# A twelve-stage decoder kernel: the context's rotation moved into a later stage, the first attention's decays as a square, a reordered cross attention of layer 0, and a query rotation packed to 128 partitions

## Chip, cores and metric

The program runs on one core of one Trainium2 chip. The metric is the device time of one execution in microseconds (us). Engines are called PE (TensorE), DVE (VectorE), ACT (ScalarE), POOL (GpSimd) and SP (SyncE, which issues most transfers). All large arithmetic is fp32.

## The reference, cut to what matters

A decoder of four layers with three sublayers each, every one of the form `x = x + f(layernorm(x))`, for x of (4, 256, 256) and a context of (4, 512, 64). The change touches five of them.

```python
# L0_attn: 16 heads of 16, chunks of 128, decay per head
D = exp(ld[:, None, None] * where(mask, diff, 0)) * mask
q_decay = exp(ld[None, :] * (idx + 1)[:, None])
k_decay = exp(ld[None, :] * (chunk - 1 - idx)[:, None])
scores = einsum('bchd,bshd->bhcs', qb, kb) * D[None]
# L0_xattn: 16 heads of 16, causal, on the context's first 256 rows
scores = where(causal, einsum('bhqd,bhkd->bhqk', qh, kh) / sqrt(16), finfo.min)
out = einsum('bhqk,bhkd->bhqd', softmax(scores), vh) @ Wout.T
# L1_xattn: 16 heads; both the query (192 wide) and the context (64 wide) are rotated
q_big = einsum('bshk,hkq->bshq', (hidden_q @ Wq.T).reshape(..., H, K), w_kc_q)
q_big = q_big * cos_q + rotate_half(q_big) * sin_q
kv_r = kv_c * cos_k + rotate_half(kv_c) * sin_k
scores = einsum('bhsr,bhlr->bhsl', einsum('bshq,hqr->bhsr', q_big, W_qr),
                einsum('bld,hdr->bhlr', kv_r, W_kr))
ctx_c = einsum('bhsl,bld->bhsd', softmax(scores), kv_r)
```

L1_attn (a selective scan over 96 channels with a second layernorm and a convolution ahead) is not changed in what it computes. L2_xattn and L3_xattn use the rotated context too.

## The kernel before

The stages run one after another, from `STAGES` in `program` (L3369 on). A stage is a row of blocks (`k.block()`); a block holds one list of instructions for each engine, ordered by semaphores, and ends when all its lists have ended. Ahead of each stage stands `layernorm` (L220 to L251), whose block also issues the stage's first transfers on SP (`fetch`, through `load`, L318). Inside a list an engine works strictly in the order written; nothing is reordered by a planner.

**The context.** `rotate_context` is a block of its own ahead of all stages: three transfers (L1510 to L1512), 13 DVE operations (L1519 to L1523) that rotate the context into `keys`, 16 transposes on PE (L1533), and two DVE copies (L1526) into `keysT`. Its results are first read in L1_xattn.

**L0_attn.** DVE builds the exponents `arg` (L592 to L596, 2320 columns). ACT takes `powers = exp(arg/8)` (L523) and its logarithm (L524), then Tanh of the query projections (L530), then Silu of the rest (L532, L537, L541). DVE corrects `powers` by one Newton step (L599, L601) and squares it three times (L603, L604, L605), scales the key's part (L607, `decay_done` 2) and builds the table (L608); only then it makes the queries, four times L613, L616, L617. PE's projections (L405, L413) go through 6 PSUM banks: the seventh waits until the first query has been taken (`took_q`). Behind them stand the low-rank gate projection (L418), which waits for no bank, its second half (L424), which waits for DVE's copy L619, and the state products (L430), which wait for POOL's L567 and L571; POOL waits for `decay_done`. The loop over 16 half units is L451 to L500.

**L0_xattn.** After 20 projections a loop over 16 steps s (4 batches x 4 groups of 4 heads), software pipelined by two. For each half step, 2 heads: `scores` writes two causal masks by bf16 matmuls (L742) and the scores by fp32 matmuls of 32 partitions (L756); DVE takes row maxima (L840); PE transposes them (`turn_tops`, L766); DVE adds them to the queries (`lower`, L849); `scores_again` computes the transposed scores with the maximum taken off (L742 again, L784); ACT takes exponentials (L892, 768 columns); `values` multiplies them with the values (L795, four column groups of 32) ; ACT keeps the sums (L898); `turn_sums` transposes them (L807) and DVE normalises (L856, L857), all inside the loop. `project_out` follows.

**L1_attn, first block.** DVE: second layernorm (L1335 to L1347), scaling out of PSUM (L1354), convolution (L1361 to L1364), the gate's product (L1369, L1371), a copy (L1374). PE: transposes (L1410), input projection (L1416), two small projections (L1421, L1425). ACT: Tanh (L1397), later Abs, Exp, Ln. POOL has nothing there. In the loop behind it POOL adds (L1477) while DVE works (L198 and on).

**L1_xattn (`latent_attention` with `rope`).** A block folds weights: `Cm` from W_qr and W_kr (L1604, 32 matmuls), `Bm` (L1612), and `Em` (L1625) in four groups, taken out of PSUM by ACT (L1655, L1658) and DVE (L1668, L1671). Weights "first" and "second" are fetched in the layernorm's block, "third" to "fifth" in this one. The next block rotates: 32 items m (8 head pairs x 2 column halves x 2 heads). `widen(m)` makes two halves of 96 rows of a head's query (L1696, 4 matmuls), DVE multiplies them with cosines and sines (L1730, L1732, 4 operations of 96x512), `narrow(m)` contracts the four products to 64 rows (L1707, 4 matmuls); the two heads of a pair follow one another. The loop is `widen(m)`, then `narrow(m-1)`:

```python
for m in range(len(items) + 1):
    if m < len(items):
        widen(m)
    if m >= 1:
        narrow(m - 1)
```

ACT copies the result to `qT` (L1741). The attention over the context follows (L1796 to L1915) and is the same code in L2_xattn and L3_xattn.

## Time and profile before

| what | us |
|---|---|
| median of 3 runs | 3408.3 |
| the runs | 3388.36, 3408.3, 3412.52 |
| the profiled execution, its own time | 3433.46 |
| its span, first to last instruction | 3431.6 |
| mean granted TensorE clock over the span | 0.819 |
| PE, DVE, ACT, POOL busy | 2704.5, 1804.5, 981.2, 799.5 |

The profile is of one execution. "Busy" is the time in which an engine executes; matmuls are pipelined and their ends are modelled, so that starts are the safer reading. PEclk is the granted clock as a share of 2.4 GHz; its two levels are 1.00 and 0.50. L12 is line 12 of the kernel before. An fp32 matmul appears as two MATMUL rows. In brackets stands how long the engine sat idle before the instruction and what ended that.

### The profile page before, as it was taken

The page shows a single profiled execution, that of the slowest core. Times are in us where ns is not written, and L with a number is a line of the kernel's source. Part 1 is how long each engine was busy: PE and PEld are TensorE (multiplying, and loading weights), DVE is VectorE, ACT ScalarE, POOL GpSimd, SP SyncE. Part 2 cuts the span into 40 slices and gives each one's busy share as a digit, 9 for nine tenths or more (in the row PEclk, how much of TensorE's full clock was granted, in tenths as well). Part 3 has the DMA queues.
Part 4 walks back from the last instruction along what each step waited for, and adds up shares of the span by engine and source line. Part 5 has one row for each costly group of instructions (what it writes and reads, how often), then busy time and mean ns, then how long its engine had stood idle before and what let it go on. Part 6 is the DMA issues. An engine that isn't in the chain of part 4 may idle for free. (4 is left out here: it accounts for less than half of the span.)

```text
span 3431.6 us, 37431 instructions
## 1 busy us (share of the span) xinstructions
PE 2704.5 (79%) x14214; PEld 1753.0 (51%) x14214; DVE 1804.5 (53%) x3596; ACT 981.2 (29%) x2209; POOL 799.5 (23%) x565
## 2 busy tenths in 40 slices
PE   4799634265999998967787869688998765899899
PEld 2555332122433555545676757475555744555555
DVE  5422568698333655348475665742554755255511
ACT  2121101153000554113423333331554111255410
POOL 1130000022000886220000000000885000188422
PEclk9765556566999999978787878877999975799899
DMA  1000000001100001021000000102001001100211
GB/s 39 16 18 1 19 0 1 3 0 48 43 0 0 1 1 51 1 100 23 3 13 13 13 13 1 25 21 66 1 1 38 0 18 44 42 1 1 77 50 40
DMA packets 96634, 72.72 MB, mean 21 GB/s; under 512 B 51248, under 2 KB 89952, under 8 KB 95881
## 3 DMA queue, kind: packets, MB, share of 16 engines
q1 hardware_dynamic: 95433, 68.88, 7.2%
q8 instruction: 114, 1.87, 0.2%
q0 software_dynamic: 1024, 1.45, 0.2%
q14 instruction: 63, 0.52, 0.0%
HBM read 65.04 MB, written 5.28 MB: 20 GB/s over the span
## 5 line engine op out<-in xcount | busy, mean ns | idle before, releaser
L1915 POOL TENSOR_SCALAR work<-work,small 128x512 f32<-128x512 f32 x384 | 593.1, 1562 | 912.3 <-DVE small L1851 912.1
L1893 ACT ACTIVATE work<-psum,small 128x512 f32<-128x512 f32 x384 | 260.2, 683 | 251.7 <-DVE small L1846 251.7
L1846 DVE TENSOR_REDUCE small<-psum 128x2 f32<-128x1024 f32 x192 | 234.8, 1224 | 178.3 <-PE psum L1796 178.2
L1796 PE MATMUL psum<-keysT,arena_a 64*128 64x512 f32 x768 | 217.1, 644 | 9.1 <-ACT work L1893 6.2
L1806 PEld LDWEIGHTS psum<-consts,work 128*128 128x128 f32 x1536 | 164.5, 141 | 114.8 <-issue 99.9
L1806 PE MATMUL psum<-consts,work 128*128 128x128 f32 x1536 | 210.9, 280 | 5.4 <-DVE work L1857 2.6
L1818 PE MATMUL psum<-work,keys 128*64 128x256 f32 x1536 | 186.9, 384 | 35.3 <-issue 34.0
L1818 PEld LDWEIGHTS psum<-work,keys 128*64 128x64 f32 x1536 | 120.0, 136 | 135.1 <-issue 109.1
L2704 PE MATMUL psum<-xnT,arena_a 128*128 128x256 f32 x512 | 154.4, 463 | 29.1 <-DVE arena_b L3084 29.1
L1477 POOL TENSOR_TENSOR arena_b<-arena_b 96x1024 f32<-96x1024 f32 x16 | 37.6, 2348 | 591.3 <-DVE arena_b L1470 591.3
L1441 PE MATMUL psum<-arena_b,arena_a 96*96 96x512 f32 x128 | 92.8, 895 | 72.5 <-DVE arena_b L1470 38.1
L2704 PEld LDWEIGHTS psum<-xnT,arena_a 128*128 128x128 f32 x512 | 117.1, 237 | 55.7 <-DVE arena_b L3084 31.2
L1857 DVE COPY work<-psum 128x512 f32<-128x512 f32 x192 | 130.7, 681 | 19.8 <-PE psum L1806 19.8
L1730 DVE TENSOR_TENSOR arena_a<-psum,work 96x512 f32<-96x512 f32 x96 | 62.8, 681 | 146.0 <-PE psum L1696 146.0
L2677 POOL TENSOR_TENSOR work<-arena_b 128x512 f32<-128x512 f32 x32 | 33.3, 1039 | 439.6 <-ACT arena_b L2965 408.5
L1900 ACT ACTIVATE work<-psum 128x512 f32<-128x512 f32 x192 | 114.3, 595 | 73.1 <-PE psum L1806 73.1
L2281 PE MATMUL psum<-xnT,arena_b 128*128 128x512 f32 (+1 forms) x272 | 121.7, 601 | 0.0
L1696 PE MATMUL psum<-xnT,arena_b 128*96 128x512 f32 x256 | 117.3, 601 | 1.6 <-PEq L72 1.6
L1707 PE MATMUL psum<-arena_a,arena_b 96*64 96x512 f32 x256 | 115.7, 598 | 0.0
L251 PE MATMUL psum<-consts,xn 128*128 128x128 f32 x192 | 43.7, 420 | 86.7 <-DVE xn L232 86.7
L840 DVE TENSOR_REDUCE work<-psum 128x2 f32<-128x256 f32 x64 | 32.7, 554 | 134.2 <-PE psum L756 134.2
L3084 DVE SCALAR_TENSOR_TENSOR work<-psum,conv_w,work 128x255 f32<-128x255 f32 (+2 forms) x192 | 83.1, 476 | 36.7 <-ACT work L2959 34.1
(576 smaller groups left out, 5222.5 us busy)
## 6 DMA issues: line engine op xcount, KB each, us to landing
arena_a<-in_L_xattn_Wo SPq DMA_DIRECT2D x3, 2048.0 KB, 12.5
arena_a<-in_L_xattn_Wq SPq DMA_DIRECT2D x3, 2048.0 KB, 17.5
arena_a<-in_L_xattn_w_kc_q SPq DMA_DIRECT2D x3, 1536.0 KB, 11.7
arena_a<-in_L_attn_w_qkv SPq DMA_DIRECT2D x1, 4096.0 KB
arena_a<-in_L_xattn_W_qr SPq DMA_DIRECT2D x3, 768.0 KB
arena_b<-in_L_ffn_w_fc SPq DMA_DIRECT2D x1, 2048.0 KB
arena_b<-in_L_ffn_w_proj SPq DMA_DIRECT2D x1, 2048.0 KB
arena_a<-in_L_attn_w_gate SPq DMA_DIRECT2D x1, 2048.0 KB
```

The source lines that it names most:

```text
L1696: mm = nc.tensor.matmul(ps[0:QH, m % 2 * 2 + q, :], Em[:, c, 2 * i + j, q * QH:(q + 1) * QH], xnT[:, c, n * 512:(n + 1) * 512], start=c == ...
L1707: mm = nc.tensor.matmul(ps[j * DC:(j + 1) * DC, 4 + g % 4, :], Cm[:, c_at(2 * i + j), z // 2, :], prods[m % 2][:, z, :], start=z == 0, sto ...
L1796: mm = nc.tensor.matmul(ps[:, u % 2 * 2 + j, :], qT[r:r + DC, p, t * P:(t + 1) * P], k.keysT[r:r + DC, b * SK:(b + 1) * SK], start=True, s ...
L1806: mm = nc.tensor.transpose(ps[:, 4 + j, c * P:(c + 1) * P], probs[u % NPB][:, j, c * P:(c + 1) * P], k.c["ident"])
L1818: mm = nc.tensor.matmul(ps[j * DC:(j + 1) * DC, 6, 0:S], k.keys[:, 4 * b + c, :], PT[q % 2][:, j, c], start=c == 0, stop=c == 3)
L1846: nc.vector.tensor_reduce(top[:, 2 * u:2 * u + 2], ps[:, u % 2 * 2:u % 2 * 2 + 2, :], AX.X, ALU.max, negate=True).then_inc(*maxed.up())
L1857: nc.vector.tensor_copy(PT[u // 2 % 2][:, 0, :, u % 2, :], ps[:, 4, :].rearrange("p (c n) -> p c n", c=4)).then_inc(*kept_d.up())
L1893: nc.scalar.activation(probs[u % NPB][:, j, :], ps[:, u % 2 * 2 + j, :], ACT.Exp, bias=top[:, i:i + 1], accum_out=total[:, i:i + 1]).then_ ...
L1900: nc.scalar.activation(PT[u // 2 % 2][:, 1, :, u % 2, :], ps[:, 5, :].rearrange("p (c n) -> p c n", c=4), ACT.Copy).then_inc(*kept_a.up())
L1915: nc.gpsimd.tensor_scalar(probs[u % NPB][:, j, :], probs[u % NPB][:, j, :], total[:, i:i + 1], None, ALU.mult).then_inc(*scaled.up())
L2281: mm = nc.tensor.matmul(ps[0:n_f, 4 + g % 2 * 2 + z, :], gu[:, c, z, i * P:i * P + n_f], xnT[:, c, n * 512:(n + 1) * 512], start=c == 0, s ...
L2704: mm = nc.tensor.matmul(ps[:, n % 3, j * S:(j + 1) * S], w_qkv[:, c, f:f + P], xnT[:, c, b * S:(b + 1) * S], start=c == 0, stop=c == 1)
```

## The change

Five edits in one.

- The context is no longer rotated in a block of its own. Its three transfers are issued in the layernorm of L1_attn behind that stage's own; POOL does the 13 operations in L1_attn's first block (`context_rotate`), PE the 16 transposes behind the input projection (`context_turn`), ACT two copies of 64x2048 behind Tanh (`context_keep`); the third small projection waits for them.
- L0_attn: `powers = exp(arg/2)`, squared once. ACT's four Tanh stand ahead of Exp and Ln, DVE's query operations ahead of the decays, and the square, `k_decay` and the table behind the copy of the gate.
- L0_xattn: scores of step s and scores again of step s-2 are issued together, alternately, on four different row groups; masks of both ahead. PSUM banks have fixed roles; `values` writes 128 columns a matmul (three a head instead of two). The sums are kept for all steps and transposed and normalised in a block behind the loop.
- L1_xattn, fold: `Cm` becomes `CmA` (128 rows) and `CmB` (64 rows), from a rearranged copy `w_cut` of W_qr that POOL makes; `Bm` is computed first; `Em` is written in two parts.
- L1_xattn, rotation: 16 units (head pair, column half) with three banks: 128 of the 192 rows of each head, and the remaining 64 rows of both heads together. 6 matmuls, 6 DVE operations of 128x512 with a table that has the sign in it, 8 narrow matmuls that alternate between the two heads' column halves.

```diff
@@ L0_attn, ACT
-            act.wait_ge(*decays.at(1))
-            k.link(act, nc.scalar.activation(powers, arg, ACT.Exp, scale=0.125), "act")
+            for i in range(4):
+                act.wait_ge(*proj.at(i + 1))
+                nc.scalar.activation(q[...], ps[:, i % 6, :], ACT.Tanh, scale=0.5).then_inc(*tanhed.up())
+            act.wait_ge(*decays.at(1))
+            k.link(act, nc.scalar.activation(powers, arg, ACT.Exp, scale=0.5), "act")
...
@@ L0_attn, DVE, behind the four query groups
+            dve.wait_ge(*k.sig("logs").at(1))
+            (arg = 0.5 * arg - logs; powers = (arg + 1) * powers)
             dve.wait_ge(*low.at(1))
             nc.vector.tensor_copy(t1..., ps[0:HD, 6:8, :]).then_inc(*put.up())
+            nc.vector.tensor_tensor(powers, powers, powers, ALU.mult).then_inc(*k.sig("decay_done").up())
+            (k_decay, decay_done; table)
@@ L0_xattn, PE
+            def both(s, half):
+                ask, again = s < Q, 0 <= s - 2 < Q
+                q, other = s - 2, 1 - half
+                first, second = FIRST[half], SECOND[other]
+                if ask:
+                    b, g = divmod(s, G)
+                    if s >= 1:
+                        pe.wait_ge(*maxed.at(2 * (s - 1) + half + 1))
+                    if half == 1 and s >= 1:
+                        pe.wait_ge(*lowered.at(s))
+                    for j in range(2):
+                        hide_later(first + j, 0)
+                if again:
+                    if q >= 1:
+                        pe.wait_ge(*expd.at(2 * (q - 1) + half + 1))
+                    if other == 0 and s >= 3:
+                        pe.wait_ge(*kept.at(s - 2))
+                    pe.wait_ge(*lowered.at(q + 1))
+                    for j in range(2):
+                        hide_later(second + j, 1)
+                for i in range(2):
+                    for j in range(2):
+                        if ask:
+                            r, (a, e), t0 = 64 * half + 32 * j, ((0, 1), (1, 3))[i], b * S
+                            mm = nc.tensor.matmul(ps[:, first + j, a * P:e * P], qT[r:r + 32, ...], kT[r:r + 32, ...], ...)
+                        if again:
+                            r, (a, e), t0 = 64 * other + 32 * j, ((0, 2), (2, 3))[i], q // G * S
+                            mm = nc.tensor.matmul(ps[:, second + j, a * P:e * P], kT[r:r + 32, ...], low_q[q % 3][r:r + 32, ...], ...)
+            for s in range(Q + 3):
+                both(s, 0)
+                if s >= 3:
+                    values(s - 3)
                 if 1 <= s <= Q:
                     turn_tops(s - 1)
+                both(s, 1)
...
@@ L1_attn, first block
             act: nc.scalar.activation(u, conv, ACT.Tanh, scale=0.5)
+            context_keep(k, act)
             pe: (input projection)
+            context_turn(k, pe)
             pe.wait_ge(*lowed.at(1))
+            pe.wait_ge(*k.sig("keys_kept").at(1))
+        @block.gpsimd
+        def _(pool):
+            context_rotate(k, pool)
@@ L1_xattn, rotation, PE
+                def widen(u):
+                    for bank, col in ((0, 0), (2, 2 * P), (1, P)):
+                        for c in range(2):
+                            mm = nc.tensor.matmul(ps[:, u % 2 * 3 + bank, :], Em[:, c, i, col:col + P],
+                                                  xnT[:, c, n * 512:(n + 1) * 512], start=c == 0, stop=c == 1)
+                def narrow(u):
+                    for v in range(2):
+                        for j in range(2):
+                            nc.tensor.matmul(ps[j * DC:(j + 1) * DC, 6 + u % 2, :], CmA[:, c_at(2 * i + j), v, :],
+                                             prods[u % 2][:, j, v, :], start=v == 0, stop=False)
+                    for v in range(2):
+                        for j in range(2):
+                            r = slice(j * DC, (j + 1) * DC)
+                            mm = nc.tensor.matmul(ps[r, 6 + u % 2, :], CmB[r, i, v, :], prods[u % 2][r, 2, v, :],
+                                                  start=False, stop=v == 1)
```

## Rows read from the trace of the kernel before

**Rows 1.** The page, section 1: busy time, share of the span and instructions of each engine.
```profile
PE 2704.5 (79%) x14214; PEld 1753.0 (51%) x14214; DVE 1804.5 (53%) x3596; ACT 981.2 (29%) x2209; POOL 799.5 (23%) x565
```
**Rows 2.** Busy time by stretches: length, PE, PEld, DVE, ACT, POOL, PEclk, DMA share, GB/s.
```profile
128.00:136.00 8.00, 7.45 (x74) 5.15 (x72) 5.44 (x6) 0.63 (x1) 0.00 (x0) 1.00 0.01 2
187.30:197.90 10.60, 10.59 (x33) 5.90 (x32) 0.69 (x1) 7.29 (x11) 8.16 (x9) 1.00 0.23 62
198.60:378.60 180.00, 176.78 (x960) 96.78 (x960) 44.75 (x112) 33.31 (x49) 6.88 (x7) 0.50 0.02 5
...
884.40:1113.90 229.50, 228.75 (x512) 71.49 (x512) 79.38 (x128) 9.55 (x16) 0.00 (x0) 1.00 0.00 0
1113.90:1356.00 242.10, 223.95 (x1408) 135.01 (x1408) 140.88 (x230) 129.02 (x322) 197.69 (x128) 1.00 0.00 1
```
**Rows 3.** Timeline of the rotation, one item: start, duration, engine, line, shapes, count.
```profile
1002.75 3.67 PE L1696 MATMUL psum<-xnT,arena_b 128*96 128x512 f32 x8
...
1006.36 3.65 PE L1707 MATMUL psum<-arena_a,arena_b 96*64 96x512 f32 x8
```
**Rows 4.** Timeline, the context's block: its first transfer, and the first of the next stage.
```profile
6.99 0.37 SPq L1510 DMA_DIRECT2D work<-in_ctx  x1
...
25.25 0.34 SPq L318 DMA_DIRECT2D arena_a<-in_L_attn_log_decay  x1
```
**Rows 5.** Timeline of L1_attn: its first block, and L198 alone and beside POOL.
```profile
644.99 1.06 ACT L1397 ACTIVATE arena_b<-arena_a 96x1024 f32<-96x1024 f32 x1 [19.84 <-DVE arena_a L1364]
...
653.11 3.72 PE L1425 MATMUL psum<-arena_a 6*96 6x512 f32 x4 [1.37 <-DVE arena_a L1374]
...
699.31 1.28 DVE L198 SCALAR_TENSOR_TENSOR work<-arena_b,arena_a,work 96x1024 f32<-96x1024 f32 x1
...
825.34 2.34 POOL L1477 TENSOR_TENSOR arena_b<-arena_b 96x1024 f32<-96x1024 f32 x1 [6.20 <-DVE arena_b L1470]
826.36 2.40 DVE L198 SCALAR_TENSOR_TENSOR work<-arena_b,arena_a,work 96x1024 f32<-96x1024 f32 x1
```
**Rows 6.** Timeline of L0_attn around the projections.
```profile
35.92 10.54 PE L405 MATMUL psum<-xnT,arena_a 128*128 128x512 f32 x24 [1.05 <-PEq L72]
...
44.40 2.23 ACT L524 ACTIVATE arena_a<-arena_a,consts 128x2320 f32<-128x2320 f32 x1
...
51.87 2.58 DVE L603 TENSOR_TENSOR arena_a<-arena_a 128x2320 f32<-128x2320 f32 x1
...
62.85 5.30 PE L405 MATMUL psum<-xnT,arena_a 128*128 128x512 f32 x8 [16.39 <-DVE arena_b L613]
...
82.08 1.21 DVE L619 COPY arena_b<-psum 16x1024 f32<-16x1024 f32 x1 [11.74 <-PE psum L418]
...
87.31 3.78 PE L430 MATMUL psum<-work 128*128 128x128 f32 x16
```
**Rows 7.** Timeline of L0_xattn's loop, parts of a step.
```profile
300.87 0.61 PE L742 MATMUL psum<-arena_b 128*128 128x256 bf16 x2
...
301.40 1.65 PE L756 MATMUL psum<-arena_a 32*128 32x128 f32 x8
...
303.60 1.51 PE L795 MATMUL psum<-work,arena_a 128*32 128x256 f32 x16
...
304.04 0.41 DVE L849 TENSOR_TENSOR work<-psum,arena_a 128x256 f32<-128x256 f32 x1
```
**Rows 8.** Timeline of L0_attn's loop: the same kind of pair in the stretch from 128 us.
```profile
131.07 1.13 PE L451 MATMUL psum<-arena_a,work 32*128 32x256 f32 x8
```
**Rows 9.** Timeline of L1_xattn's attention, PE alone.
```profile
1200.27 1.95 PE L1818 MATMUL psum<-work,keys 128*64 128x256 f32 x16 [0.39 <-issue]
...
1203.17 1.13 PE L1796 MATMUL psum<-keysT,arena_a 64*128 64x512 f32 x4
```
**Rows 10.** Timeline of L1_xattn's fold, two PE groups.
```profile
854.13 5.41 PE L1604 MATMUL psum<-arena_a 64*96 64x64 f32 x64 [1.05 <-PEq L72]
...
869.37 13.44 PE L1625 MATMUL psum<-arena_a 128*128 128x192 f32 x64 [5.29 <-issue]
```

More of the change, by code:

```diff
@@ L1607, in _, with outputs @@
-            mm.then_inc(*fold.up())
-            k.wait_weights(pe, "second")
-            for h in range(H):
-                r, i = h % 2 * DC, h // 2
-                mm = nc.tensor.matmul(ps[r:r + DC, 4 + i // 2, i % 2 * D:(i % 2 + 1) * D], w_v[:, h, :], wo[:, h, :],
-                                      start=True, stop=True)
-            mm.then_inc(*fold.up())
+            def outputs():
+                k.wait_weights(pe, "second")
+                for h in range(H):
+                    r, i = h % 2 * DC, h // 2
+                    mm = nc.tensor.matmul(ps[r:r + DC, 4 + i // 2, i % 2 * D:(i % 2 + 1) * D], w_v[:, h, :], wo[:, h, :],
+                                          start=True, stop=True)
+                mm.then_inc(*fold.up())
@@ new lines, in _ @@
+            k.wait_weights(pe, "first")
+            if rope:
+                outputs()
+                pe.wait_ge(*k.sig("ready").at(1))
+                for h in range(H):
+                    r, a = h % 2 * R, c_at(h)
+                    for v in range(2):
+                        mm = nc.tensor.matmul(ps[:, a // 4, (a % 4 * 2 + v) * DC:(a % 4 * 2 + v + 1) * DC],
+                                              w_cut[r:r + R, h // 2, v, 0:P], w_kr[r:r + R, h // 2, :], start=True, stop=True)
+                mm.then_inc(*fold.up())
+                pe.wait_ge(*taken.at(1))
+                for h in range(H):
+                    r, a = h % 2 * R, h // 2
+                    for v in range(2):
+                        mm = nc.tensor.matmul(ps[r:r + R, 4 + a // 4, (a % 4 * 2 + v) * DC:(a % 4 * 2 + v + 1) * DC],
+                                              w_cut[r:r + R, h // 2, v, P:Q], w_kr[r:r + R, h // 2, :], start=True, stop=True)
+                mm.then_inc(*fold.up())
+            else:
+                for h in range(H):
+                    r = h % 2 * R
+                    for c in range(2):
+                        a = c_at(h)
+                        mm = nc.tensor.matmul(ps[0:QH, a // 4, (a % 4 * 2 + c) * DC:(a % 4 * 2 + c + 1) * DC],
+                                              w_qr[r:r + R, h // 2, c * QH:(c + 1) * QH], w_kr[r:r + R, h // 2, :],
+                                              start=True, stop=True)
+                mm.then_inc(*fold.up())
+                outputs()
@@ L1645, in _ @@
                 mm.then_inc(*fold.up())
+        if rope:
+            @block.gpsimd
+            def _(pool):
+                k.wait_weights(pool, "first")
+                halves = w_qr.rearrange("p h (z d) -> p h z d", z=2)
+                for v in range(2):
+                    for z in range(2):
+                        nc.gpsimd.tensor_copy(w_cut[:, :, v, 64 * z:64 * z + 64], halves[:, :, (z + v) % 2, 0:64])
+                        last = nc.gpsimd.tensor_copy(w_cut[:, :, v, P + 32 * z:P + 32 * z + 32], halves[:, :, (z + v) % 2, 64:QH])
+                last.then_inc(*k.sig("ready").up())
         @block.scalar
@@ L1680, in latent_attention @@
     if rope:
-        prods = [A.take(QH, 4, 512) for _ in range(2)]
+        prods = [A.take(P, 3, 2, 512) for _ in range(2)]
         rotated = k.sig("rotated")
+        units = [divmod(u, 2) for u in range(2 * HP)]
         with k.block() as block:
@@ L1686, in _ @@
             def _(pe):
-                items = [(i, n, j) for i in range(HP) for n in range(2) for j in range(2)]
-                def widen(m):
-                    i, n, j = items[m]
-                    if m >= 2:
-                        pe.wait_ge(*rotated.at(m - 1))
-                    for q in range(2):
+                def widen(u):
+                    i, n = units[u]
+                    if u >= 2:
+                        pe.wait_ge(*rotated.at(u - 1))
+                    for bank, col in ((0, 0), (2, 2 * P), (1, P)):
@@ L1717, in _ @@
+                for u in range(2 * HP + 1):
+                    if u < 2 * HP:
+                        widen(u)
+                    if u >= 1:
+                        narrow(u - 1)
             @block.vector
@@ L1737, in _ @@
             def _(act):
[L1738 to L1742 removed]
+                for u in range(2 * HP):
+                    i, n = units[u]
+                    act.wait_ge(*k.sig("mm_out").at(u + 1))
+                    nc.scalar.activation(qT[:, i, n * 512:(n + 1) * 512], ps[:, 6 + u % 2, :], ACT.Copy).then_inc(*taken.up())
     else:
```

377 lines of the change are left out of this document (159 added, 218 removed).

## Prediction

> **What bounds the kernel now.** I read the page first, then the busy time by stretches, then the order of instructions in the five places that the diff touches. The page shows no engine that is the limit everywhere: PE is busy 79% of the span, DVE 53% [rows 1]. The program is twelve stages, each with blocks that end in a barrier, so the average says little; each edit has to be priced in its own stage, between the barriers that close it. Two of the five places are waits: from 6.99 to 25.25 us the context's rotation, a block of its own behind which all stages stand [rows 4], and 16.4 us in L0_attn in which PE is idle and DVE's L613 ends it [rows 6]. The other two show in the stretches [rows 2]: from 198.6 to 378.6 us (cross attention of layer 0) PE is busy 176.8 of 180.0 us, at a granted clock of 0.50 throughout, the lower level, 1.2 GHz. In 884.4 to 1113.9 us (rotation of the queries of layer 1) PE is busy 228.75 of 229.5 us at 1.00, 2.4 GHz, and DVE only 79.4. So there PE's own instructions are the bound, and only fewer, or more of them side by side, or a higher clock can shorten them.
>
> A measure used below: an fp32 matmul is two MATMUL rows. Eight rows of 512 columns, one after the other, take 3.61 us to the start of the next group [rows 3]; I put 0.43 each, 3.44, down to streaming (0.84 ns a column at 2.4 GHz, so 1.67 ns at 1.2 GHz) and the other 0.17 us to the change of shape.
>
> **Part 1, the context.** Its block ran from 6.99 to 25.25 us [rows 4], with nothing else in it; the next stage starts 18.3 us earlier. What it did goes into the first block of L1_attn and its layernorm. Three transfers are added behind eleven others on SP's queue; that queue has nothing else to do in the layernorm. POOL gets 13 instructions. 96x1024 takes it 2.34 us [rows 5], so I estimate 0.6 us for each of 4 of 256 elements, 0.3 for each of 8 of 128, 2.3 for the last: 7.1 us, from the block's start at about 620 to 628. PE's 16 transposes (3.8 us like the 16 of L430, [rows 6]) stand behind the input projection, while DVE does its convolution, which ends at 645.0. ACT's two copies of 64x2048 (I estimate 1.9 us each, from 1.06 for 1024 columns) stand behind Tanh, 646.05 to 649.9; the matmul that waits for them would start at 653.11 [rows 5]. All hidden, with some 3 us to spare. What is not hidden is POOL beside DVE: the same DVE instruction takes 1.28 us alone and 2.40 us while POOL works [rows 5]. DVE's chain of small operations in the second layernorm lies just there. I take 1.5 us; the ends are 0 and POOL's whole 7.1. A gain is possible too: 16 more transposes may let PE's two 3.6 us groups run at 2.4 GHz, up to 3.6 us. Term: -16.8 (from -22 to -11).
> The Trainium skill, SBUF — State Buffer, "Who interferes with whom", speaks against this placement: a DVE instruction with two SBUF inputs and a GpSimd instruction that reads SBUF exclude each other for a whole instruction. By that rule the loss is at most POOL's own time, so a term between -18.3 and -11.2; the 1.28 against 2.40 us agree with it.
>
> **Part 2, the decays.** Now ACT's Tanh for the queries stands behind Exp and Ln (2.2 us each), and DVE's product behind five operations of 2320 columns (2.58 us each) and the table; PE waits 16.39 us for DVE's L613 [rows 6]. After: the sixth projection ends at 46.4 (six in 10.54 us, 1.72 each), and by then DVE, free since 39.6 when the exponents are made, has taken the first query and freed the seventh's bank. The next wait could be for the key's Silu: Tanh until 43.5, then Exp, Ln and three table loads (I estimate 1.3 each from the gaps between them), Silu at 52.3; PE needs that bank at 53.1. So PE runs through 14 projections and the low-rank one (3.6) to 63.7, where it now ends at 82.05 [rows 6]. What is late next is POOL's key decay: PE needs the two squares' result through decay_done. DVE: copy 63.7 to 65.0, one square to 67.6, then POOL's two products of 1024 columns, 2.34 each by the row of L1477 [rows 5], to about 72.3. PE's L430, which started at 87.31, starts at about 72.3: 15.0 us. POOL's first product and DVE's table (2.3) now overlap and may cost each other a microsecond or two; if ACT's path slips it costs as much. Term: -15 (from -17 to -11). Of the two dropped multiplications (5.2 us) only one would have lain on this path.
>
> **Part 3, cross attention of layer 0.** Its 16 steps with their ends take 180.0 us, 11.25 each [rows 2]. L756 (32 partitions, two row groups) is 4x128+4x256 columns, 2.57 us if serial; it took 1.65 [rows 7], so its two row groups run side by side (1.28). L795 is (8x256+8x128) columns, 5.1 us serial, and took 1.51: four column groups side by side. The change issues four row groups together, two of `ask`, two of `again`, 384 columns each. A half then costs four masks (0.21 each at 1.2 GHz by their 256 bf16 columns, 0.85) + 1.28 + about 0.4 for changes of shape = 2.5 us, in place of two halves of 2.1 (L742 to L756 0.53, L756 1.6, [rows 7]). A step at 1.2 GHz: 2x2.5, values 1.5, tops 0.6, and a wait that is new: the second half's masks wait for lower(), which waits for the tops just issued, 0.1+0.41+0.1 = 0.6 us. Together 7.8 us. At 2.4 GHz by the shapes that ran there (8 rows of L451 in 1.13 us where two side by side stream 0.86, [rows 8]): half 0.43+0.64+0.3 = 1.37, values 0.85 (half of 1.5 and 0.1), tops 0.45, wait 0.6: 4.7 us. DVE (44.75/16 = 2.8 us a step now) and ACT (33.31/16 = 2.1) stay below either [rows 2].
> Which clock? PE was busy all along at 1.2 GHz with two row groups; with one group of 64 rows (187.3 to 197.9) and with pairs that fill the array (1113.9 to 1356) it was at 2.4 [rows 2]. The new step does the same work in 70% of the time even at 1.2 GHz, so I take 2.4 after the first steps. Loop: 17 steps' worth x 4.7 = 80, first steps at the lower clock 11, and the new block behind it (32 transposes, four pairs of DVE operations, a barrier) an estimated 7, from 3.8 us for 16 such [rows 6]: 98 against 180. Term: -82 (from -97, all at 2.4, to +5, below).
> The Trainium skill, TensorE: Matmul & The Clock Gate, Part 3, "Measured speedup vs the span model", gives 3.07, not 4, for four row groups. By that 0.64 becomes 0.83 and the term -75 (an estimate of mine from that page). No run here shows four row groups together.
>
> **Part 4, rotation of layer 1.** Before: 229.5 us for 32 items, 7.17 each, of which widen 3.61 and narrow 3.56 [rows 3]. After: 16 units; widen 12 rows at 0.43 = 5.16; narrow 8 rows with 128 partitions by 64 columns and 8 of 64 by 64, each in pairs on different halves. L1818 has the first shape: 16 rows of 256 columns, 3.45 us serial, 1.95 measured; L1796 has row pairs: 1.13 us where serial is 1.72 [rows 9]. So 1.72+1.72, and three changes of shape 0.45: 9.05 us, x16 = 145. DVE has 79.38/128 = 0.62 us an operation, 6 a unit, 3.7 us, and is hidden [rows 2]. Term: -84 (serial pairs: 12.5 us, 200, -29; at best -87).
> In front of it the fold grows. CmA's weights have 128 columns where L1604's have 96, at 5.41/64 = 0.085 us each [rows 10]; 64 x 0.11 = 7.2 us, CmB 64 x 0.058 = 3.7, together 10.9 in place of 5.4. Now PE waits 5.29 us for weights, until 869.37; after, outputs() can start when Wo has landed (by 859.5, when L1604 ends and its matmuls run now; I take 858), takes 4.6, then 10.9: 873.5. POOL's w_cut (8 copies, about 4 us) is hidden behind outputs(). With split evacuations +4 (from +1 to +6).
>
> **Sum.** -16.8 -15 -82 -84 +4 = -194 us. The profiled execution took 3433.5 us (span 3431.6), so 3239.5 for it; it was 25 us above the median of the three runs, 3408.3, for which the same sum gives **3214 us**.
>
> **Rivals.**
> (A) The loop of layer 0 stays at 1.2 GHz. For: it never left 0.50 in 180 us. Against: the work is now denser. 17x7.8+9 = 142, term -38: 3258 us. 20%.
> (B) The 64-column pairs of the rotation run one after another, since the 512-column form and the mix of three shapes in a unit are not in the trace. Term -29: 3269 us. 7%.
> (C) The change doesn't do what it says: four row groups in the order j, j' don't overlap, only two do. Half 3.8 us at 1.2 GHz, step 10.3, 175+10 = 185, +5: 3301 us. 7%.
> (D) Slower: the narrow shapes in the rotation let the clock fall, and it stays down through the attention behind it. At 1.2 GHz a unit takes 17.6 us, 282 (+52), and the 242.1 us of attention, with PE busy 224, lose up to 200: 3214+84+52+200 = 3550 us. With the other terms it turns slower once the attention loses over some 58 us, a quarter of its stretch at 1.2 GHz. Against: the same shapes held 1.00 [rows 2]. 2%.
> My forecast 64%. The range 3175 to 3285 holds it, A and B and the bounds of parts 1 and 2; C, D and a still better loop are left out. A measurement of this kernel tells about 1%, 34 us, from no change; all but D and an odd remainder are faster by more: 0.96, 0.02, 0.02.
>
> **What would show it.** Right: first stage's DMA issue at 7 us; no PE idle of 16 us near 30 to 45; a step of about 4.7 us in the layer 0 loop with PEclk 1.00; rotation of about 145 us with L1818-like pairs; w_dt's matmul in L1_attn not waiting for ACT. Wrong: a loop step of 8 us or more, a narrow part over 4 us, or a rotation below clock 1.00.

## The result, and the profile after it

| | before | after |
|---|---|---|
| median of the runs, us | 3410.41 (4 runs, 3388.36 to 3430.91) | 3240.18 (4 runs, 3237.0 to 3245.44) |
| ratio, 95% interval | | 0.9503 (0.9442 to 0.9565) |
| the profiled execution, us | 3433.46 (span 3431.6) | 3245.44 (span 3243.6) |
| mean granted clock of it | 0.819 | 0.829 |

170 us less by the medians, 188 by the profiled executions (after's profiled execution is one of its four runs, before's is a fifth). Every stage begins with its first transfer on SP, so the starts of those rows split both spans (in us; the last column is what the prediction gave):

| stage | before | after | difference | predicted |
|---|---|---|---|---|
| ahead of L0_attn | 25.25 | 7.25 | -18.0 | -18.3 |
| L0_attn | 134.25 | 121.78 | -12.5 | -15 |
| L0_xattn | 231.50 | 144.80 | -86.7 | -82 |
| L1_attn | 234.01 | 237.72 | +3.7 | +1.5 |
| L1_xattn | 511.92 | 427.55 | -84.4 | -84 +4 |
| the eight others | 2294.67 | 2304.50 | +9.8 | 0 |
| span | 3431.60 | 3243.60 | -188.0 | -194 |

The stages that the diff doesn't touch are 9.8 us longer in this one execution (L2_attn 3.9, L2_xattn 2.9, L3_ffn 2.0 of it). In the fourteen profiles of this study, those of the experiments below included, the same code in L2_attn took 816.05 to 823.33 us. That is the size of what one profile can't tell.

The page of after, section 1, and the busy time of the loop of layer 0 (its first steps, the rest, the new block behind it), of the rotation and of the attention (columns as in [rows 2]):

```profile
PE 2533.6 (78%) x14342; PEld 1696.4 (52%) x14342; DVE 1770.8 (55%) x3533; ACT 985.2 (30%) x2219; POOL 814.6 (25%) x586
...
168.44:188.22 19.78, 17.96 (x130) 10.38 (x131) 7.37 (x16) 3.95 (x5) 6.90 (x7) 0.57 0.14 37
188.22:254.90 66.68, 57.78 (x926) 41.08 (x926) 30.86 (x65) 28.34 (x43) 0.00 (x0) 1.00 0.01 2
255.66:263.62 7.96, 6.54 (x32) 6.33 (x33) 4.20 (x8) 0.00 (x0) 0.00 (x0) 0.63 0.00 0
769.98:916.10 146.12, 145.18 (x448) 50.55 (x448) 58.90 (x96) 9.58 (x16) 0.00 (x0) 1.00 0.00 1
916.10:1158.20 242.10, 225.16 (x1408) 135.42 (x1408) 140.37 (x228) 128.69 (x321) 198.03 (x128) 0.99 0.00 1
```

Against [rows 2]: the loop, 180.0 us at 0.50, is now 95.2 us with its block, at 1.00 after the first 20 us up to the block behind it; the rotation, 229.5, is 146.1. The attention behind the rotation took 242.1 us in both, at 1.00 before and 0.99 after.

The timeline of a step of that loop, which answers to [rows 7] (behind each L741 row sixteen rows of 32 partitions are left out, two for each of the eight matmuls of a half step):

```profile
225.49 0.60 PE L741 MATMUL psum<-arena_b 128*128 128x256 bf16 x4 [0.61 <-DVE work L835]
...
226.89 0.61 PE L741 MATMUL psum<-arena_b 128*128 128x256 bf16 x4
...
228.29 0.66 PE L789 MATMUL psum<-work,arena_a 128*32 128x128 f32 x16
228.75 0.42 PE L793 MATMUL psum<-work,arena_a 128*32 128x128 f32 x8
229.11 0.44 PE L801 MATMUL psum<-consts,work 128*128 128x128 f32 x2
229.58 0.42 DVE L835 TENSOR_TENSOR work<-psum,arena_a 128x256 f32<-128x256 f32 x1 [1.55 <-PE psum L801]
...
230.15 0.60 PE L741 MATMUL psum<-arena_b 128*128 128x256 bf16 x4 [0.61 <-DVE work L835]
```

From L741 to L741 the step is 4.66 us: halves of 1.40, values 0.82, tops 0.44, and 0.61 in which PE waits for `lower` (L835).

L0_attn, the timeline that answers to [rows 6]:

```profile
17.91 16.30 PE L407 MATMUL psum<-xnT,arena_a 128*128 128x512 f32 x32 [1.05 <-PEq L72]
...
44.50 3.61 PE L420 MATMUL psum<-xnT,arena_a 128*16 128x512 f32 x8
...
48.22 1.21 DVE L613 COPY arena_b<-psum 16x1024 f32<-16x1024 f32 x1 [9.46 <-PE psum L420]
...
52.03 2.28 DVE L617 SCALAR_TENSOR_TENSOR arena_a<-arena_a 128x2048 f32<-128x2048 f32 x1
52.21 4.31 POOL L568 TENSOR_TENSOR work<-arena_b,arena_a 128x1024 f32<-128x1024 f32 x1 [29.82 <-DVE arena_a L616]
...
56.48 1.93 POOL L572 TENSOR_TENSOR work<-work,arena_a 128x1024 f32<-128x1024 f32 x1
58.46 3.78 PE L432 MATMUL psum<-work 128*128 128x128 f32 x16 [5.27 <-POOL work L572]
```

The wait of 16.39 us is gone. What is late now is POOL: PE's state products (L432, before L430) wait for L572, and L568, one operation of 128x1024, took 4.31 us beside DVE's table. DVE itself had idled 9.46 us in front of its copy L613.

L1_attn, first block: DVE's last small operations of the second layernorm, beside POOL's last of the context:

```profile
509.29 0.37 DVE L192 TENSOR_TENSOR ln_rs<-ln_rs 128x8 f32<-128x8 f32 x1
509.70 0.17 DVE L193 TENSOR_TENSOR ln_rs<-ln_rs 128x8 f32<-128x8 f32 x1
509.72 2.35 POOL L1318 TENSOR_TENSOR keys<-keys,work 128x1024 f32<-128x1024 f32 x1
509.90 2.19 DVE L1385 SCALAR_TENSOR_TENSOR ln_rs<-ln_mv,ln_rs 128x8 f32<-128x8 f32 x1
```

An operation of 8 elements a partition took 2.19 us, and it ended with POOL's.

The fold, which answers to [rows 10], and one unit of the rotation, which answers to [rows 3]:

```profile
746.66 5.12 PE L1620 MATMUL psum<-arena_a 128*64 128x256 f32 x32 [6.76 <-DMA arena_a<-in_L_xattn_Wo]
751.72 3.84 PE L1631 MATMUL psum<-arena_a,work 64*128 64x64 f32 x64
...
755.48 2.13 PE L1638 MATMUL psum<-arena_a,work 64*64 64x64 f32 x64
757.54 10.67 PE L1662 MATMUL psum<-arena_a 128*128 128x192 f32 x64
...
784.18 5.42 PE L1744 MATMUL psum<-xnT,arena_b 128*128 128x512 f32 x12
...
789.52 1.94 PE L1755 MATMUL psum<-arena_a,arena_b 128*64 128x512 f32 x8
...
791.39 1.93 PE L1760 MATMUL psum<-arena_a,arena_b 64*64 64x512 f32 x8
793.25 5.42 PE L1744 MATMUL psum<-xnT,arena_b 128*128 128x512 f32 x12
```

A unit is 9.07 us. CmA (L1631) took 3.84 us and CmB (L1638) 2.13.

### The profile page after: what moved, and what is told of

It reads as the page before. It is cut to its first block and busy times, and to the rows that moved or that the text cites. A ratio compares the mean times of both kernels' runs of the same rounds, so it can differ in the third digit from the quotient of the medians.

```text
span 3243.6 us, 37597 instructions
## 1 busy us (share of the span) xinstructions
PE 2533.6 (78%) x14342; PEld 1696.4 (52%) x14342; DVE 1770.8 (55%) x3533; ACT 985.2 (30%) x2219; POOL 814.6 (25%) x586
## 5 line engine op out<-in xcount | busy, mean ns | idle before, releaser
L1779 DVE TENSOR_TENSOR arena_a<-psum,work 128x512 f32<-128x512 f32 x96 | 58.9, 683 | 82.8 <-PE psum L1744 82.8
L2384 DVE TENSOR_TENSOR arena_a<-arena_a,psum 128x512 f32<-128x512 f32 (+1 forms) x34 | 23.4, 687 | 144.0 <-ACT arena_a L2406 144.0
L1489 PEld LDWEIGHTS psum<-arena_b,arena_a 96*96 96x96 f32 x128 | 29.9, 245 | 135.9 <-issue 84.8
L1877 PE MATMUL psum<-arena_b,work 128*128 128x256 f32 x384 | 99.1, 381 | 1.6 <-DVE work L1913 1.6
L1913 DVE COPY work<-psum 128x256 f32<-128x256 f32 x96 | 40.8, 425 | 108.8 <-PE psum L1867 108.8
```

What stands on the lines that cost most here:

```text
L1489: mm = nc.tensor.matmul(ps[0:C, s % 2 * 4 + 2 * g + n, :], w, u[:, n * 512:(n + 1) * 512], start=True, stop=True)
L1877: mm = nc.tensor.matmul(ps[:, 7, t * D:(t + 1) * D], ctx[q % 2][:, t * P:(t + 1) * P], Bm[:, p, :], start=p == 0 and t == 0, stop=p == HP ...
```

## Experiments

Every run is compared with runs of the kernel before on the same chip. The kernels stand in three groups that shared those runs, with medians of before of 3388.0, 3404.4 and 3395.7 us; after itself (3240.18) is from a fourth. The ratios below compare with before. After ran beside none of these kernels, so a total that lies within 5 us of 3240.18 is not taken as a difference from it; what an edit of after did is read from its own stage, against the same stage in the profiles in which that code is as in after.

### The kernel before once more

No edit.

> The kernel before, not changed, for a second profile. The profiled execution of before took 3433 us, 23 above the median of its four runs, and the stages that the diff doesn't touch took 9.7 us less in it than in the profile of after. Theory 1: the spread is the granted clock's, spread over the stages: the five stages of the diff repeat within 3 us each (context 18, L0_attn 134.3, L0_xattn 231.5, L1_attn 234.0, L1_xattn 511.9), and what the total differs by is in others. Theory 2: the loop of L0_xattn, at 1.2 GHz throughout in the first profile, gets the higher clock for a part in the shorter executions: then its 180 us come out 15 to 25 shorter and the median's gain of 170 us, against 188 in the profiles, is explained by it.

Measured: one execution, 3434.93 us, its stages within 0.9 us of the first profile's, L0_xattn 231.60 again. The profiled executions are alike, so this run tells neither theory from the other. But the seven other executions on that chip took 3372.74 to 3434.54 us: there is something in before that goes two ways, and both profiles show the longer one.

### Part 3 undone, and part 3 alone

The function `l0_xattn` of before put into after (first), and that of after put into before (second).

> After, with the cross attention of layer 0 as before (part 3 undone, all else as in after). Both profiles of before took 3433 to 3435 us, with the loop at a granted clock of 0.50 throughout, while other executions of before took 3373 to 3412; after's lie within 3237 to 3245. Theory 1: the loop of before is what can go either way: this kernel's executions spread over 40 us or more, up to 3245+87 = 3332 (loop 180 us at 1.2 GHz) and down to about 3270 to 3290; if the profiled one is a short one, its loop shows a clock above 0.50. Theory 2: the loop is always at 1.2 GHz and the spread of before is elsewhere: all executions within 10 us of 3327. Part 3 is then worth 87 us in every execution, by theory 1 only 30 to 60 in the shorter ones.

> Before, with the cross attention of layer 0 of after and nothing else (part 3 alone). By the stages of the two profiles 3433-87 = 3346 us. Theory 1 (the loop was what spread): executions within 10 us of 3346. Theory 2 (the spread is elsewhere): they spread over 40 us or more, 3285 to 3346, as those of before do.

Measured, part 3 undone: median 3301.88 us, 3277.61 to 3322.96 in six runs, ratio to before 0.9665 (0.9594 to 0.9736). The mean clock of those executions was 0.815 to 0.817 in the three long ones and 0.823 to 0.827 in the three short ones. The profiled one (3314.95) shows the loop, and for the first time a rise in it:

```profile
168.00:320.00 152.00, 151.16 (x818) 82.89 (x818) 38.59 (x95) 26.92 (x40) 5.18 (x6) 0.50 0.02 5
320.00:340.00 20.00, 17.19 (x135) 9.93 (x134) 5.63 (x16) 5.21 (x8) 0.00 (x0) 0.76 0.00 1
```

L0_xattn took 225.17 us in it, 6 less than in before. Part 3 alone: median 3354.58, all four within 3352.03 to 3358.93, ratio 0.9832 (0.9757 to 0.9907).

So the spread goes with the old loop: the kernels that have it spread over 42 to 72 us, those with the new one over 5 to 11. The old loop was at 0.50 throughout in two profiles and rose late in a third; the new one came to 1.00 within 25 us of its start in all ten profiles that have its masks ahead, and stayed there up to its last steps. Part 3 is worth 87 us against an execution whose loop stays at 1.2 GHz. By the medians it is worth less: 62 us with part 3 undone (3301.9 to 3240.2, two groups), 60 against the next kernel below, which has the new loop and shared the runs of before, and 50 with part 3 alone (3404.4 to 3354.6, the same chip). No profile of a short execution of before was had; that its gain lies in this loop rests on the two spreads and on this one rise.

### Two row groups at a time

```diff
                 for i in range(2):
                     for j in range(2):
                         if ask:
...
+                for i in range(2):
+                    for j in range(2):
                         if again:
                             (scores again)
```

> After, with the four matmuls of the scores issued ahead of the four of the scores again in each half step, so that neighbours lie on two row groups, no longer four. Same work, same number of instructions. Theory 1 (overlap reaches only over what is issued next to one another, and the denser step is what held the clock up): two groups at a time, the loop falls to 1.2 GHz, half 3.8 us, step about 10.3, L0_xattn 144.8+90 = 235, total 3330. Theory 2 (overlap as in theory 1, but the clock stays up): half 0.7 us longer at 2.4 GHz, step 6.1, L0_xattn 168, total 3263. Theory 3 (the second pair starts beside the first all the same, because their row groups differ): step under 5 us, no change.

Measured: 3242.11 us, ratio 0.9496 (0.9423 to 0.9569), L0_xattn 145.17. Theory 3. The timeline of a half step (L768 scores, L777 scores again; in the program all eight rows of L768 stand first):

```profile
222.23 0.38 PE L768 MATMUL psum<-arena_a 32*128 32x128 f32 x2
222.25 0.48 PE L777 MATMUL psum<-work,arena_a 32*128 32x256 f32 x2
222.44 0.49 PE L768 MATMUL psum<-arena_a 32*128 32x128 f32 x4
222.57 0.38 PE L777 MATMUL psum<-work,arena_a 32*128 32x256 f32 x2
```

The fifth instruction (the first L777) started 0.02 us behind the first and 0.2 ahead of the L768 rows that follow the first two. By these starts PE took matmuls of other row groups out of their order, so the alternation that the change writes out isn't what makes four run together. The section on the kernel before says that inside a list an engine works strictly in the order written; for PE's matmuls that doesn't hold.

### Masks between, as before

```diff
-                if again:
...
-                    for j in range(2):
-                        hide_later(second + j, 1)
                 for i in range(2):
                     for j in range(2):
                         if ask:
...
+                if again:
...
+                    for j in range(2):
+                        hide_later(second + j, 1)
+                for i in range(2):
+                    for j in range(2):
                         if again:
```

The three waits of scores again went with its masks to behind the first four matmuls.

> After, with the order of before inside a half step: masks and scores of the one step, then masks and scores again of the other. The run with two groups in turn showed that order among the eight 32-row matmuls doesn't matter (the fifth instruction started 20 ns behind the first); what is left that could keep four groups apart is a matmul of 128 rows between them. Theory 1 (masks of both ahead are what lets four groups overlap, and the denser step is what lifts the clock): half 0.7 us longer at 2.4 GHz and the clock falls, step 10 to 11, L0_xattn about 230, total 3325 with executions spread over 30 us or more, as with the old loop. Theory 2 (overlap lost, clock stays): step 6.1, L0_xattn 168, total 3263. Theory 3 (PE starts the second pair past the masks): no change, 3240.

Measured: 3343.29 us (3338.16 to 3345.92), ratio 0.9856 (0.9791 to 0.9921), L0_xattn 244.19. The half step in the timeline, and the loop's stretch:

```profile
200.68 0.59 PE L741 MATMUL psum<-arena_b 128*128 128x256 bf16 x2 [0.61 <-DVE work L837]
201.19 1.65 PE L760 MATMUL psum<-arena_a 32*128 32x128 f32 x8
202.78 0.61 PE L741 MATMUL psum<-arena_b 128*128 128x256 bf16 x2
203.31 1.65 PE L777 MATMUL psum<-work,arena_a 32*128 32x256 f32 x8
204.90 0.61 PE L741 MATMUL psum<-arena_b 128*128 128x256 bf16 x2
...
168.00:346.00 178.00, 162.62 (x990) 93.31 (x990) 38.21 (x80) 30.95 (x46) 6.93 (x8) 0.50 0.02 5
```

Theory 1 for the time: the pairs run one after the other, as in [rows 7], the step is 11.2 us and the clock stays at its lower level. Its spread of 30 us did not come (8 us), so a loop at 0.50 doesn't by itself bring the spread. With the run above this names the edit inside part 3 that pays: the masks, matmuls of 128 rows, no longer stand between those that are to overlap. The waits moved with the masks. The rows show no idle time at them, but a kernel with only the masks moved wasn't run, so that the masks alone end the overlap is not shown. The clock went with the overlap: the same matmuls ran at 0.50 pair after pair and at 1.00 four together.

### The rotation's pairs in turn

```diff
-                    for v in range(2):
-                        for j in range(2):
+                    for j in range(2):
+                        for v in range(2):
```

(in both groups of `narrow`)

> After, with the rotation's narrow matmuls ordered by head first: each head's two halves of a product one after the other on the same 64 columns, in place of alternating between the heads' column halves. Theory 1 (the gain of part 4 in narrow comes from neighbours on different column halves): each of the two groups of 8 rows goes from 1.94 to 3.45 us, the unit from 9.07 to 12.1, L1_xattn 427.5+49 = 476, total 3290. Theory 2: half of the neighbours still differ (j changes once in each group), so a part overlaps all the same: unit 11 to 11.5. Theory 3: order doesn't matter: 9.07.

Measured: 3239.43 us in one execution, and in the timeline

```profile
852.43 1.95 PE L1755 MATMUL psum<-arena_a,arena_b 128*64 128x512 f32 x8
...
854.31 1.94 PE L1760 MATMUL psum<-arena_a,arena_b 64*64 64x512 f32 x8
856.18 5.42 PE L1744 MATMUL psum<-xnT,arena_b 128*128 128x512 f32 x12
```

Theory 3. Had only neighbours on different column halves overlapped, a group would have taken longer than the 1.94 us of after; so column halves, too, are taken out of order, inferred from the time alone.

### Transposes of the maxima ahead of the values

```diff
+                if 1 <= s <= Q:
+                    turn_tops(s - 1)
                 if s >= 3:
                     values(s - 3)
-                if 1 <= s <= Q:
-                    turn_tops(s - 1)
```

> After, with the transposes of the maxima issued ahead of the values in each step of the layer 0 loop, so that the 0.8 us of values cover DVE's lower. PE idled 0.61 us a step for lower, 15 times. Theory 1: the step falls from 4.66 to 4.05 us, L0_xattn 144.8 to about 135, total 3230. Theory 2 (maxed isn't ready that early and PE waits there instead): under 3 us. Theory 3: with the step shorter ACT's exponentials (2x0.8 + 0.4 us and their latencies) become the bound: 3 to 7 us.

Measured: 3237.65 us (3234.54 to 3241.34), ratio 0.9577 (0.9546 to 0.9608), L0_xattn 141.14, 3.7 less than in after and below the 144.6 to 151.2 of all profiles with after's loop. The step is 4.36 us (L801 at 222.01 and 226.37). The wait for `lower` is gone, but 0.2 to 0.3 us of another took its place: half of the masks wait until ACT has copied the sums of `values` out of PSUM (L870, 0.38 us), and `values` now stands right ahead of them. No theory had it; the size is that of theory 2.

### Squares early, and the eighth power kept

The first moves DVE's square, key decay and table ahead of the wait for the low-rank projection. The second keeps after's order and takes back the power:

```diff
-            k.link(act, nc.scalar.activation(powers, arg, ACT.Exp, scale=0.5), "act")
+            k.link(act, nc.scalar.activation(powers, arg, ACT.Exp, scale=0.125), "act")
...
+            k.link(dve, nc.vector.tensor_tensor(powers, powers, powers, ALU.mult), "dve")
+            k.link(dve, nc.vector.tensor_tensor(powers, powers, powers, ALU.mult), "dve")
             dve.wait_ge(*low.at(1))
```

(and 0.125 for 0.5 in the Newton step).

> After, with DVE's square, key decay and table moved from behind the copy of the gate to ahead of its wait. DVE idled 9.46 us in front of that copy. Theory 1 (the decays were late only by their place in DVE's order): decay_done comes at about 41.5 instead of 52.1, POOL's two products are done by about 48, and the state products start straight behind the gate's second half, 53.2 instead of 58.46: 5.3 us less in L0_attn, total 3235. Theory 2 (the end of the stage is set by the loop behind it, where the clock is low and PE waits for others): L0_attn shorter by under 2 us. Theory 3: POOL beside DVE slows DVE's copy, so that the low-rank part is late: no gain.

> After, with the decays as an eighth power again (scale 0.125, two more squarings of 2320 columns on DVE, 2.57 us each) but in after's order, the two ahead of the wait for the low-rank projection, where DVE idled 9.46 us. Theory 1 (the gain of part 2 was all from the order): the state products start as in after, 51.2 us into the stage (48.6 where the clock is up from the first projection), total 3240 within 3. Theory 2 (as the prediction had it: one of the two dropped squarings lay on the path): 2.6 us later. Theory 3: both, 5.2 us later, 3245.

Measured, squares early: 3236.53 us (3233.21 to 3238.68), ratio 0.9577 (0.9549 to 0.9606).

```profile
41.47 4.32 POOL L568 TENSOR_TENSOR work<-arena_b,arena_a 128x1024 f32<-128x1024 f32 x1 [19.34 <-DVE arena_a L614]
45.75 1.93 POOL L572 TENSOR_TENSOR work<-work,arena_a 128x1024 f32<-128x1024 f32 x1
...
52.92 3.57 PE L432 MATMUL psum<-work 128*128 128x128 f32 x16
```

The stage began at 7.01, so L432 came 45.9 us into it in place of 51.2: the 5.3 us of theory 1. The stage got 3.0 shorter (118.75), and that isn't separated from noise: with after's code it took 119.4 to 127.1 us in eight profiles, in part by its first projection (32 rows in 13.97 to 16.30 us) and in part by the clock granted behind it.

Measured, eighth power: 3244.15 us (3240.73 to 3251.3), ratio 0.957 (0.9507 to 0.9634), L0_attn 121.59, L432 50.8 us into the stage. Theory 1: two squarings of 2.57 us ahead of DVE's copy cost nothing, since 4.25 of the 9.46 us of idle time are still left. The square in the change's title brought no time; the order did. The total holds a longer L0_xattn, 151.16 us, which this edit doesn't touch (see the last experiment).

### The context's rotation later

```diff
+            pool.wait_ge(*k.sig("ln_xn").at(1))
             context_rotate(k, pool)
```

> After, with POOL's context rotation in L1_attn waiting until DVE has finished the second layernorm (8.5 us into the block). In after DVE's eight small operations took up to 0.65 us instead of 0.17, and the last one 2.19 us, which ended when POOL's operation of 1024 columns did. Theory 1 (a DVE instruction waits for a whole POOL instruction): the 3.1 us that the layernorm lost come back, DVE's next operations read PSUM and lie 3 us apart, so about 3 us less in L1_attn (237.7 to 234.7), total 3237. Theory 2 (the loss only moves: POOL now collides with the scaling out of PSUM and the convolution): 0 to 1 us. Theory 3: the transposes become late and PE's w_dt waits: longer by 1 to 3 us.

Measured: 3236.77 us (3233.84 to 3238.92), ratio 0.9578 (0.955 to 0.9606), L1_attn 234.39, 3.3 less, as theory 1 has it (237.4 to 238.6 in the nine profiles with after's code). The operation that took 2.19 us and the start of POOL:

```profile
506.47 0.17 DVE L1385 SCALAR_TENSOR_TENSOR ln_rs<-ln_mv,ln_rs 128x8 f32<-128x8 f32 x1
...
509.43 0.72 POOL L1314 TENSOR_TENSOR keys<-work 128x256 f32<-128x256 f32 x1 [334.66 <-DVE arena_a L1388]
```

POOL's operations, up to the start of its last (515.59, 2.34 us), now lie beside DVE's L1395 (513.20), which reads PSUM and took 2.96 us for four, against 2.97 in before and after.

### CmA ahead of outputs

```diff
-                outputs()
                 pe.wait_ge(*k.sig("ready").at(1))
...
                 mm.then_inc(*fold.up())
-                pe.wait_ge(*taken.at(1))
+                outputs()
+                pe.wait_ge(*taken.at(2))
```

(ACT and DVE take the results out of PSUM in the new order, too.)

> After, with the fold's CmA ahead of outputs() (the order of before), CmB behind it. In after PE waited for Wo until 16.0 us into the stage, and CmA and CmB took 3.84 and 2.13 us, not the 7.2 and 3.7 of the prediction. Theory 1 (they were short because outputs() had run just ahead of them and the clock was up; in front, they run at 1.2 GHz): CmA 6.5 to 7.5 us from 13.8 us into the stage, so that outputs() starts at 20.5 to 21.5 instead of 16.0, Em 3 to 4 us later, L1_xattn 430 to 431. Theory 2 (a matmul of 128 by 64 by 64 costs 0.06 us at either level): CmA 3.9 us, hidden in the wait for Wo but for 2 us, Em 2 us earlier or equal.

Measured: 3247.1 us in one execution, L1_xattn 430.66, 3.1 longer (426.2 to 427.6 in the ten profiles with after's order). The stage began at 732.17:

```profile
746.21 7.11 PE L1630 MATMUL psum<-arena_a,work 64*128 64x64 f32 x64 [4.81 <-POOL work L1692]
...
753.26 5.98 PE L1620 MATMUL psum<-arena_a 128*64 128x256 f32 x32
...
762.95 10.67 PE L1662 MATMUL psum<-arena_a 128*128 128x192 f32 x64
```

Theory 1: the same 64 rows take 7.11 us at a granted clock of 0.50, when PE has just been idle for 4.81 us, and 3.84 at 1.00 behind outputs(), and Em starts 30.8 us into the stage, not 26.9.

### Three edits together

Squares early, context late, maxima first.

> After with three edits that each gave a part: squares, key decay and table ahead of the copy of the gate (state products 5.3 us earlier), context rotation behind the second layernorm (L1_attn 3.3 us shorter), transposes of the maxima ahead of the values (L0_xattn 3.7 us shorter). If they add up, stages of 116.5 to 119, 141.1 and 234.4, total about 3228 (3223 to 3232) against 3240 of after. Theory 2: the gain in L0_attn is given back by its loop, in which the clock is low: total 3231 to 3235.

Measured: 3235.39 us (3232.37 to 3239.83, six runs), ratio 0.9537 (0.9491 to 0.9583). Not 3228. L1_attn kept its gain (234.09). L0_attn took 122.88 although L432 came at 46.35: the gate's second half took 6.52 us, not 3.7, at a granted clock of 0.56, and the loop behind it ran at 0.71, in after at 0.75.

```profile
46.91 6.52 PE L426 MATMUL psum<-arena_b,arena_a 16*128 16x512 f32 x8 [1.38 <-DVE arena_b L618]
53.35 3.78 PE L432 MATMUL psum<-work 128*128 128x128 f32 x16
```

L0_xattn took 146.85, with the first maxima on DVE (L825) 3 to 5 us late while POOL still issued its indirect transfers. All four kernels of this group (masks between, eighth power, CmA ahead and this one), which ran on one chip, show that, and none of the ten other profiles does, so it isn't an effect of these edits; why it comes is open. Beside the two of the group that have after's loop, 151.16 and 149.00 us, the 146.85 are still 2 to 4 less. The version may be some us better than after; it wasn't run beside it, so no more can be said.

## Why the prediction was right, and where it was wrong

The text said 3214 within 3175 to 3285; 3240 came, in the range and 26 us above. The case that it called likeliest came, and no rival: four row groups and the column halves overlapped, and the clock rose.

**The step that failed is the last line of the sum**: "it was 25 us above the median of the three runs, 3408.3, for which the same sum gives 3214". The sum itself, -194 on the profiled execution, gave 3239.5 for it, and 3245.44 came: its five stages gave -197.8, and the eight others were 9.8 longer. (That 3239.5 also lies at the measured median is chance.) But what set the profiled execution above the median isn't independent of the change. It goes with the loop of layer 0 that part 3 replaces: with part 3 undone the times spread over 45 us, with part 3 alone put in over 7. In the median execution of before a part of part 3's 87 us was already there. With the 62 us of part 3 undone the stages give -18.0 -12.5 -62 +3.7 -84.4 = -173, with the 50 of part 3 alone -161; -170 was measured. So the term's worth on the median is between 50 and 62, in place of 82. The spread of the runs and the 0.50 of [rows 2] were both in sight; the mistake was to take the one for noise.

**Part 1** (-16.8; -14.3 came). The 18 us are right. Hidden, as said: PE's transposes (1.91 us, at the higher clock, in place of 3.8) and ACT's copies (3.73 us for two, estimated 3.8; w_dt's matmul didn't wait for them). The 1.5 us for POOL beside DVE was too small: 3.1 in the layernorm alone, beside POOL operations that took 8.5 us together, estimated 7.1. The three rows of L1385 (2.19 beside POOL, 0.17 as L1344 in before, 0.17 with POOL later) show a DVE operation that stands until POOL's has ended. The rest is mostly the input projection, 6.69 us for 5.88, at a granted clock of 0.53 for 0.62. The rule of the Trainium skill that the prediction weighed (SBUF — State Buffer, "Who interferes with whom": exclusion for a whole instruction) agrees with this trace, 2.19 us beside POOL's 2.35, and the loss of 3.1 lies between the 1.5 that was taken and the 7.1 that bounded it.

**Part 2** (-15; -12.5). L432 came 51.2 us into its stage, before 62.1: 10.9 at that point. Two things make up the rest: POOL's L568 took 4.31 us, not 2.34, because DVE's table lay beside it, at the upper end of the "microsecond or two" of the text; and the first 32 rows took 16.30 us, the first of them up to 1.19 us each, twice the 0.59 of the others. In five of the ten later profiles the same rows took 13.97, in the other five 15.65 to 16.35; what decides it is open. Behind L432 the stage was 1.6 us shorter than in before. "Of the two dropped multiplications only one would have lain on this path" is wrong: by the run with the eighth power neither did.

**Part 3** (-82; -86.7). Step by step: half 1.40 (said 1.37), values 0.82 (0.85), tops 0.44 (0.45), wait for `lower` 0.61 (0.6), step 4.66 (4.7). First steps and tail together took 86.5 us and the block 8.0, said 91 and 7. The other 2 us are the output projection, 10.2 us at 1.00 for 12.4 at 0.80. Rival A would have needed the step at 1.2 GHz; the run with the masks between shows that this rival was near: with half of the masks and their waits behind the first pair the loop stays at 0.50. Rival C named the order j, j' as what could fail; that order didn't matter, but where the masks of 128 rows stood did. Four groups of 384 columns are 2.58 us in a row by 0.84 ns a column and row, and the four took 0.87 to the next mask, a factor of 3.0, changes of shape included. The 3.07 of the Trainium skill (TensorE: Matmul & The Clock Gate, Part 3, "Measured speedup vs the span model") agrees with that.

**Part 4** (-84 and +4; -84.4). Rotation 229.5 to 146.1 (said 145), unit 9.07 (9.05), both groups of narrow at 1.94. The fold was +4 in the text and came to -1.6: the rotation began 39.3 us into the stage, before 40.9. Its CmA term, 7.2 us, was scaled from the row of L1604, which ran at 0.50, and 7.11 was measured with CmA in front; behind outputs(), at 1.00, it is 3.84, CmB 2.13 for 3.7, and Em, 13.44 before, 10.67. Wo arrived 16.0 us into the stage, said 14.5. Rival B didn't come, in either order of the matmuls. Rival D didn't either: the rotation ran at 1.00 and the attention behind it at 0.99.

0.96 was put on faster, and it came.

## What to carry to other kernels

Before a sum made on a profiled execution is carried over to the median, ask which stage makes that execution long, and whether the change replaces it: a stretch that PE fills at the lower clock in one execution may run in part at the higher in others, and the gain on the median is then smaller. To let small matmuls run side by side, collect those on different row groups or column halves between the ones that use the whole array; their order among themselves made no difference here. A move to POOL beside DVE is priced by the length of POOL's single instructions against DVE's small ones: where a chain of them lay there, the loss was 3.1 of POOL's 8.5 us.

## What the runs showed of the hardware that was not expected

- PE starts matmuls on different row groups out of program order: the fifth instruction 0.02 us behind the first (two groups at a time); for column halves it is inferred from the same 1.94 us in either order. The Trainium skill, TensorE: Matmul & The Clock Gate, Part 3, "The mechanism", says that matmuls start and end strictly in program order and only weight loads are pulled ahead; the starts in this trace differ from that.
- With two masks of 128 rows, and their waits, between the pairs there was no overlap (step 11.2 us, clock 0.50); with all four ahead there was (4.66 us, 1.00).
- A DVE operation of 8 elements a partition took 2.19 us beside a POOL operation of 2.35, and a POOL operation of 128x1024 took 4.31 beside DVE's table of 2.28, the next of its size, with DVE idle, 1.93.
- The old loop was at 0.50 throughout in two profiles and at 0.76 for 20 us near its end in a third. The six executions of that third kernel took 3277.61 to 3322.96 us at mean clocks of 0.815 to 0.827, with nothing in the program that differs; that the short ones rose earlier in this loop is likely and not shown.
